# A DLRM tower with ten one-hot tables, gram samples 27 columns apart, whole-bank gram evictions and gram writes by tile

## The chip, the cores and the metric

The kernel runs on one NeuronCore of a Trainium2 chip. The metric is the device time of one execution in microseconds. The core's engines are TensorE (PE in the profile, with its weight loads as PEld), VectorE (DVE), ScalarE (ACT), GpSimd (POOL) and SyncE (SP).

## What is computed

For 2048 samples, 27 rows of 128 numbers are looked up in 27 tables, the 27 × 26 / 2 = 351 dot products of their pairs are formed, and three dense layers follow:

```python
e = jnp.stack([tbl_0[ids[:, 0]], ..., tbl_26[ids[:, 26]]], axis=1)        # 2048 x 27 x 128
interactions = jnp.einsum('bfd,bgd->bfg', e, e).reshape(B, F * F)
z = jnp.concatenate([bottom, interactions[:, TRIL_IDX]], axis=1)          # 128 + 351
h = jnp.concatenate([z, bottom], axis=1)                                  # 607
h = jnp.maximum(h @ W_top1 + b_top1, 0.0)                                 # 512
h = jnp.maximum(h @ W_top2 + b_top2, 0.0)                                 # 256
y = h @ W_top3                                                            # 1
```

Twelve tables have 1000 rows, nine 1250, five 12500 and one 125000. Everything is float32.

## The kernel before

**Halves and tiles.** The batch is worked through in 8 halves of 256 samples (0 to 7; FIRST and LAST in the code), each of two tiles of 128. Halves 0, 1 and 7 are written out, 2 to 6 run in a loop. The dense layers of half i − 1 run inside half i.

**Lookups.** 18 tables are gathered: GpSimd issues one indirect DMA a table and tile (`gather`, L372 to L382), 18 in a run, in groups of four tables, into `rows`. There is one buffer a tile, so the run for tile t of half i + 1 begins when TensorE has transposed the first four tables of tile t of half i (the wait on `built`, L376). TensorE transposes the gathered rows into `embT` (`transpose_tile`, L720). The other 9 tables, all of 1000 rows, stay in SBUF, split into a high and a low part, and are looked up by products with one-hot matrices: VectorE compares ids with row numbers (`make_hot`, L401; a part is 4 instructions of 125 × 256, there are two parts a table and so 18 a half), TensorE multiplies (`onehot_unit`, L702; 8 matmuls a part). Tables go in pairs, the units; unit 4 has one table. The one-hots lie in a ring of `HOT_SLOTS` = 6 parts: part a is made when TensorE has used part a − 6 (L408 to L413). So six parts of the next half are made ahead, inside this half, and 12 are left to its start.

**Order of a half.** `features`: units 0 to 4, with the transposes of tile 0 between them. `first_tile`: pair products of tile 0, u = 0 to 3. `second_rows`: dense layer 1 of the half before (m = 0 to 3), with the transposes of tile 1 between. `second_tile`: pair products of tile 1, with layers 2 and 3 between.

**Pair products.** A matmul takes 4 samples at once: stationary are their 27 columns each, samples 32 apart in `embT`, so 122 columns; moving are their columns 1 to 26, 104 (`pair_products`, L726). 16 matmuls fill two PSUM banks: that is one product u. Two such pairs of banks take turns, so product u ≥ 2 waits until product u − 2 is evicted (L735 to L737). Only the blocks of one sample with itself are of use. Each eviction (`empty_gram`, L420 and L546) copies four of them, 32 partitions × 208: two on VectorE, two on ScalarE, into `gram`, which holds a half.

**Pairs to dense.** When the half is evicted, SyncE writes `gram` to DRAM in two DMAs (`write_gram`, L304) and reads it back feature by sample with 29 DMAs (`read_pairs`, L311), in pieces of 256 bytes. `pairs_high` and `pairs_low` split them in three chunks for layer 1; on ScalarE and VectorE they stand behind the evictions of u = 0, 1, 2 of tile 0. The last half doesn't go through DRAM but is transposed by TensorE.

**SyncE's queue in a half** (`half`, L322): ids of unit 3, gram writes, ids of unit 4, 29 reads, ids of unit 2 for the next half, bottom rows, ids of units 0 and 1 for the next half, store of y. Each load of ids waits until the one-hots from its buffer are made.

## Time and profile before

| | us |
|---|---|
| median of 3 runs | 683.68 |
| lowest, highest | 678.6, 684.86 |
| the profiled execution | 678.93 |
| its span in the profile | 677.1 |
| mean granted TensorE clock | 0.785 of full |

A page of the profile shows one execution: busy times of the engines, DMA queues, the chain of work that ended last, and groups of instructions by source line. The other views are timelines (instructions in order of time, merged where alike), the same chain in order of time, and DMA packets in a stretch. A duration of TensorE's matmuls is modelled, their starts are recorded; when the result is seen to be done is told by the start of whoever waits for it.

### The profile page before, as it was taken

What the parts mean: (1) busy time and instruction counts of PE and PEld (TensorE: products, weight loads), DVE (VectorE), ACT (ScalarE), POOL (GpSimd) and SP (SyncE); (2) the same over time, 40 slices, a digit from 0 to 9 for tenths busy, and PEclk for the clock granted to TensorE, in tenths of its full rate; (3) what the DMA queues carried; (4) which work ended last, traced back from release to release, by engine and by line L of the source; (5) the groups of instructions that cost most, each with busy time, mean ns of one, the idle gap of its engine ahead of it and who ended that gap; (6) DMA issues with size and microseconds to landing.
All of it is one profiled execution on the core that took longest, in us unless ns stands there. A gap on an engine that the chain in (4) does not pass through costs nothing.

```text
span 677.1 us, 9154 instructions
## 1 busy us (share of the span) xinstructions
PE 454.0 (67%) x3110; PEld 430.6 (64%) x3110; DVE 250.0 (37%) x797; ACT 168.6 (25%) x393; POOL 319.0 (47%) x295
## 2 busy tenths in 40 slices
PE   2506575975499274983849838498384974749997
PEld 2406574974488173982849837398373974749987
DVE  5508032932075030741317313173222712228423
ACT  1203121333022040321312213122131212212454
POOL 6775545586607646085450854508454283630000
PEclk9857785985689586985858968698695975859999
DMA  6944512261122301232112341124311261112100
GB/s 165 234 100 90 138 28 58 77 104 44 51 71 63 85 25 47 72 68 78 31 39 72 74 71 31 39 73 73 71 35 35 76 90 51 39 31 78 25 1 1
DMA packets 38113, 44.51 MB, mean 66 GB/s; under 512 B 20127, under 2 KB 30887, under 8 KB 38090
## 3 DMA queue, kind: packets, MB, share of 16 engines
q1 hardware_dynamic: 27251, 23.54, 16.9%
q0 software_dynamic: 9216, 18.89, 10.5%
q10 hardware_dynamic: 1623, 1.79, 1.0%
q8 instruction: 13, 0.21, 0.1%
q14 instruction: 10, 0.08, 0.0%
HBM read 38.50 MB, written 5.69 MB: 65 GB/s over the span
## 4 chain that ended last, share of the span: by engine, by line
PE 45%; another core or an unknown queue 24%; issue 15%; DVE 11%; ACT 2%; DMA 1%; SPq 1%; DVEq 0%; ACTq 0%
PE ps_gram L741 18%; PE ps_dense L750 11%; PE ps_build L714 11%; DVE hot L416 8%; PE ps_build L724 2%; DVE table L395 1%; DMA raw<-tbl_dram 1%; PE ps_dense L787 1%; DVE gram L425 1%; PE ps_gram L750 1%; ACT embT L544 1%; PE ps_gram L724 1%; PE ps_build L750 0%; SPq L277 0%
## 5 line engine op out<-in xcount | busy, mean ns | idle before, releaser
L380 POOL DMA_INDIRECT rows<-tbl_dram,idx x288 | 318.2, 1105 | 281.2 <-issue 110.2
L741 PE MATMUL ps_gram<-embT 128*122 128x104 f32 x1024 | 173.9, 339 | 119.3 <-issue 51.4
L741 PEld LDWEIGHTS ps_gram<-embT 128*122 128x122 f32 x1024 | 163.8, 253 | 129.5 <-issue 77.4
L714 PE MATMUL ps_build<-hot,table 125*128 125x256 f32 x1152 | 154.9, 293 | 46.8 <-issue 32.2
L714 PEld LDWEIGHTS ps_build<-hot,table 125*128 125x128 f32 x1152 | 147.3, 199 | 49.3 <-issue 48.1
L416 DVE TENSOR_SCALAR hot<-id_raw,vocab 125x256 fp32r<-125x256 int32 x576 | 160.8, 354 | 31.4 <-remote 25.5
L425 DVE COPY gram<-ps_gram 32x208 f32<-32x208 f32 x128 | 46.7, 365 | 268.0 <-remote 182.2
L551 ACT COPY gram<-ps_gram 32x208 f32<-32x208 f32 (+1 forms) x128 | 41.4, 324 | 236.1 <-remote 163.3
L750 PE MATMUL ps_dense<-h,w2s 128*128 128x256 f32 x168 | 36.6, 371 | 40.6 <-issue 40.4
L750 PEld LDWEIGHTS ps_dense<-h,w2s 128*128 128x128 f32 x168 | 31.4, 270 | 43.7 <-issue 43.7
L537 ACT COPY embT<-ps_build 128x512 f32<-128x512 f32 (+1 forms) x40 | 24.9, 622 | 135.8 <-PE ps_build L714 79.7
L395 DVE TENSOR_TENSOR h<-ps_dense,h 128x256 fp32r<-128x256 f32 x28 | 11.9, 424 | 101.4 <-ACT h L574 71.3
L750 PE MATMUL ps_dense<-pairT,w1p 120*128 120x256 f32 (+1 forms) x252 | 39.1, 300 | 5.0 <-issue 5.0
L750 PEld LDWEIGHTS ps_dense<-pairT,w1p 120*128 120x128 f32 (+1 forms) x252 | 36.2, 209 | 4.4 <-issue 4.4
L572 ACT ACTIVATE ps_dense<-ps_dense,b1s 128x256 f32<-128x256 f32 x28 | 12.6, 449 | 76.1 <-remote 53.8
L724 PE MATMUL ps_build<-ident,rows 128*128 128x128 f32 x144 | 22.4, 290 | 4.5 <-ACT embT L544 2.6
L724 PE MATMUL ps_gram<-ident,rows 128*128 128x128 f32 x144 | 22.1, 276 | 2.5 <-issue 2.3
L544 ACT COPY embT<-ps_gram 128x512 f32<-128x512 f32 (+1 forms) x40 | 21.5, 545 | 6.7 <-remote 2.9
L544 ACT COPY embT<-ps_build 128x512 f32<-128x512 f32 (+1 forms) x40 | 20.4, 551 | 8.9 <-remote 8.0
L724 PEld LDWEIGHTS ps_build<-ident,rows 128*128 128x128 f32 x144 | 17.6, 149 | 7.5 <-issue 7.4
L750 PE MATMUL ps_dense<-botT,w1b 128*128 128x256 f32 x84 | 19.1, 340 | 0.0
L724 PEld LDWEIGHTS ps_gram<-ident,rows 128*128 128x128 f32 x144 | 16.8, 142 | 3.5 <-issue 3.5
(58 smaller groups left out, 139.2 us busy)
## 6 DMA issues: line engine op xcount, KB each, us to landing
id_raw<-ids_onehot_dram SPq DMA_DIRECT2D x32, 256.0 KB
rows<-tbl_dram,idx POOLq DMA_INDIRECT x288
gram_dram<-gram SPq DMA_DIRECT2D x7, 624.0 KB
raw<-tbl_dram SPq DMA_DIRECT2D x9, 448.0 KB
gram_dram<-gram SPq DMA_DIRECT2D x7, 169.0 KB
id_raw<-ids_onehot_dram SPq DMA_DIRECT2D x8, 128.0 KB
bot<-bottom_dram SPq DMA_DIRECT2D x8, 128.0 KB
w1p_raw<-w_pairs_dram ACTq DMA_DIRECT2D x1, 720.0 KB
```

The source lines that it names most:

```text
L380: nc.gpsimd.indirect_dma_start(rows[:, t, s * D:(s + 1) * D], None, tables[f], bass.IndirectOffsetOnAxis(idx[:, 2 * i + t, f:f + 1], 0)).t ...
L395: return nc.vector.tensor_tensor(dst, whole, high.bitcast(fp32), ALU.subtract)
L416: last = nc.vector.tensor_scalar(hot[0:VP, a % HOT_SLOTS, v, :], id_raw[0:VP, n % ID_SLOTS, q, :], vocab[0:VP, row:row + 1], None, ALU.is_ ...
L425: last = nc.vector.tensor_copy(*gram_pieces(t, u, k))
L537: nc.scalar.copy(embT[:, :, f:f + n], src).then_inc(emb_done, 1)
L544: nc.scalar.copy(embT[:, t * TILE:(t + 1) * TILE, u * FQ:u * FQ + n], src).then_inc(emb_done, 1)
L551: last = nc.scalar.copy(*gram_pieces(t, u, k))
L572: nc.scalar.activation(bank, bank, ACT.Relu, bias=b1s[:, m:m + 1]).then_inc(relu_done, 1)
L714: last = nc.tensor.matmul(bank[:, q * HALF:(q + 1) * HALF], table[0:VP, units[n][q], bits, row:row + D], hot[0:VP, a % HOT_SLOTS, v, :], s ...
L724: last = nc.tensor.transpose(bank[:, f * 128:(f + 1) * 128], rows[:, t, s * D:(s + 1) * D], ident[:, :])
L741: last = nc.tensor.matmul(ps_gram[u % 2][0:GR, c:c + GC], embT[:, at:at + GROUP, :].rearrange("p k g -> p (k g)")[:, 0:GR], embT[:, at:at ...
L750: last = nc.tensor.matmul(bank, w(a), x(b), start=(first and m == 0), stop=(end and m == 2))
```

## The change

- A tenth table is looked up by one-hots: 20 parts a half for 18, 17 gathers a tile for 18. Unit 4 has two tables.
- `HOT_SLOTS` is 5 for 6. Five parts of the next half are made ahead and 15 are left to its start: one instead of two beside layer 1, one behind each eviction of tile 1 as before.
- In halves 0 to 6 samples lie 27 apart in `embT` for 32; the stationary side has 107 columns (4 × 27 − 1) for 122, the moving side 104 as before. The last half keeps the old layout.
- An eviction there is one copy an engine: VectorE takes the whole first bank (107 × 416), ScalarE the whole second, off-diagonal blocks included. `gram` now holds one tile.
- Gram writes go by tile, four DMAs (one a sample of the four) of 26 partitions × 3328 bytes. Those of tile 0 are issued at the end of SyncE's half, ahead of the store of y. The first eviction of tile 1 waits for them, the first of the next tile 0 for those of tile 1.
- The 29 reads have pieces of 128 bytes for 256, eight a row for four.
- The DMA descriptor scratch is 4096 bytes a partition for 8192. In the startup one more table is loaded and split.
- The order of samples in `bottom` and `y` follows the new layout; that costs no work.

```diff
-ONEHOT_TABLES = 9
+ONEHOT_TABLES = 10
-    HOT_SLOTS = 6
+    HOT_SLOTS = 5
+    JT = TILE // GROUP
+    GM = GROUP * FEATURES - 1
...
-        gram = in_arena("gram", [GR, PG, J], fp32, 0)
+        gram = in_arena("gram", [GM, GROUP, PG, JT], fp32, 0)
+        gram_end = in_arena("gram_end", [GR, PG, J], fp32, 0)
...
+        emb_flat = sb("embT", [128, HALF * PAD], fp32)
+        embT_end = emb_flat.rearrange("p (b g) -> p b g", g=PAD)
+        embT = emb_flat[:, 0:HALF * FEATURES].rearrange("p (b g) -> p b g", g=FEATURES)
...
+        TILE_OUT = 16 * GROUP
+        def gram_bank(u, h):
+            src = ps_gram[u % 2][0:GM, h * 512:h * 512 + GB // 2 * GC].rearrange("p (g c) -> p c g", c=GC)
+            j = u * GB + h * GB // 2
+            return gram.rearrange("p k n j -> p (k n) j")[:, :, j:j + GB // 2], src
...
-            def write_gram(i):
-                sp.wait_ge(gram_dve, GRAMS * (i + 1))
-                sp.wait_ge(gram_act, GRAMS * (i + 1))
+            def write_gram(i, t):
+                sp.wait_ge(gram_dve, GRAMS * i + GU * (t + 1))
+                sp.wait_ge(gram_act, GRAMS * i + GU * (t + 1))
                 sp.sem_inc(loads_begun, 1)
-                for a, b in ((0, 96), (96, GR)):
-                    sp.dma_start(scratch[a:b, :], gram[a:b, :, :].rearrange("p n j -> p (n j)")).then_inc(gram_out, 16)
+                for k in range(GROUP):
+                    src = gram[k * FEATURES:k * FEATURES + PG, k, :, :].rearrange("p n j -> p (n j)")
+                    sp.dma_start(scratch[t * GROUP + k, :, :, :].rearrange("r n j -> r (n j)"), src).then_inc(gram_out, 16)
...
             def half(i, at, more=True):
                 next_ids(i, 0, at, 3)
-                write_gram(i - 1)
+                write_gram(i - 1, 1)
                 next_ids(i, 1, at, 4)
                 read_pairs(i - 1, range(len(reads)))
...
                     next_ids(i, 3, at + HALF, 0)
                     next_ids(i, 4, at + HALF, 1)
+                    write_gram(i, 0)
                 store(i - 1, at - HALF)
...
             def empty_gram(i, t, u):
-                if t == u == 0 and not is_half(i, FIRST):
-                    dve.wait_ge(gram_out, 32 * i)
+                if u == 0 and t == 0 and not is_half(i, FIRST):
+                    dve.wait_ge(gram_out, TILE_OUT * 2 * i)
+                if u == 0 and t == 1 and not is_half(i, LAST):
+                    dve.wait_ge(gram_out, TILE_OUT * (2 * i + 1))
                 dve.wait_ge(grammed, GRAMS * i + t * GU + u + 1)
-                for k in (0, 1):
-                    last = nc.vector.tensor_copy(*gram_pieces(t, u, k))
-                last.then_inc(gram_dve, 1)
+                if is_half(i, LAST):
+                    nc.vector.tensor_copy(*gram_pieces(t, u, 0))
+                    nc.vector.tensor_copy(*gram_pieces(t, u, 1)).then_inc(gram_dve, 1)
+                else:
+                    nc.vector.tensor_copy(*gram_bank(u, 0)).then_inc(gram_dve, 1)
...
-                    if more and m < 2:
-                        make_hot(i + 1, m)
+                    if more and m == 0:
+                        make_hot(i + 1, 0)
                 for u in range(GU):
                     empty_gram(i, 1, u)
                     if more:
-                        make_hot(i + 1, 2 + u)
+                        make_hot(i + 1, 1 + u)
...
-                        last = nc.tensor.matmul(ps_gram[u % 2][0:GR, c:c + GC],
-                                                embT[:, at:at + GROUP, :].rearrange("p k g -> p (k g)")[:, 0:GR],
-                                                embT[:, at:at + GROUP, 1:FEATURES], start=True, stop=True)
+                            last = nc.tensor.matmul(ps_gram[u % 2][0:GM, c:c + GC],
+                                                    embT[:, at:at + GROUP, :].rearrange("p k g -> p (k g)")[:, 0:GM],
+                                                    embT[:, at:at + GROUP, 1:FEATURES], start=True, stop=True)
...
-    nc = _bacc.Bacc("TRN2", target_bir_lowering=False, num_devices=1, dynamic_dma_scratch_size=8192)
+    nc = _bacc.Bacc("TRN2", target_bir_lowering=False, num_devices=1, dynamic_dma_scratch_size=4096)
...
-    args["scratch"] = nc.dram_tensor("gram_dram", (128, PG * J), _mybir.dt.float32, kind="Internal").ap()
+    args["scratch"] = nc.dram_tensor("gram_dram", (2 * GROUP, PG, PG, TILE // GROUP), _mybir.dt.float32, kind="Internal").ap()
```

## Rows read from the trace of the kernel before

**Rows 1.** The page: busy time and share of each engine; the gathers' DMA queue.

```profile
PE 454.0 (67%) x3110; PEld 430.6 (64%) x3110; DVE 250.0 (37%) x797; ACT 168.6 (25%) x393; POOL 319.0 (47%) x295
...
q0 software_dynamic: 9216, 18.89, 10.5%
```

**Rows 2.** The chain that ended last, in order of time (start, us, what), half 4.

```profile
379.05 14.69 issue
```

**Rows 3.** Timeline of POOL, half 4 (start, us, engine, line, what, idle before).

```profile
372.23 7.64 POOL L380 DMA_INDIRECT rows<-tbl_dram,idx  x1 [22.35 <-PE ps_gram L724]
380.17 0.94 POOL L380 DMA_INDIRECT rows<-tbl_dram,idx  x1 [0.30 <-PE ps_gram L724]
...
400.15 0.94 POOL L380 DMA_INDIRECT rows<-tbl_dram,idx  x1 [0.30 <-issue]
412.29 0.94 POOL L380 DMA_INDIRECT rows<-tbl_dram,idx  x1 [11.20 <-PE ps_build L724]
...
433.52 0.94 POOL L380 DMA_INDIRECT rows<-tbl_dram,idx  x1 [0.30 <-issue]
```

**Rows 4.** Timeline of DVE, half 4.

```profile
368.46 10.59 DVE L416 TENSOR_SCALAR hot<-id_raw,vocab 125x256 fp32r<-125x256 int32 x40
393.74 0.74 DVE L425 COPY gram<-ps_gram 32x208 f32<-32x208 f32 x2 [14.69 <-issue]
...
404.38 0.74 DVE L425 COPY gram<-ps_gram 32x208 f32<-32x208 f32 x2 [9.09 <-remote]
...
437.91 0.74 DVE L425 COPY gram<-ps_gram 32x208 f32<-32x208 f32 x2 [4.39 <-remote]
```

**Rows 5.** Timeline of PE, half 4.

```profile
363.07 7.91 PE L714 MATMUL ps_build<-hot,table 125*128 125x256 f32 x64
...
384.88 5.31 PE L741 MATMUL ps_gram<-embT 128*122 128x104 f32 x32 [2.33 <-ACT embT L544]
...
405.18 3.62 PE L741 MATMUL ps_gram<-embT 128*122 128x104 f32 x16 [7.01 <-DVE gram L425]
```

**Rows 6.** Timelines of POOL, PE and DVE, half 1.

```profile
134.76 2.67 POOL L380 DMA_INDIRECT rows<-tbl_dram,idx  x1 [0.30 <-issue]
137.73 1.83 POOL L380 DMA_INDIRECT rows<-tbl_dram,idx  x1 [0.30 <-issue]
...
157.70 0.94 POOL L380 DMA_INDIRECT rows<-tbl_dram,idx  x1 [0.30 <-issue]
162.21 0.94 POOL L380 DMA_INDIRECT rows<-tbl_dram,idx  x1 [3.57 <-PE ps_build L724]
...
139.69 8.72 PE L741 MATMUL ps_gram<-embT 128*122 128x104 f32 x64 [3.06 <-ACT embT L544]
...
142.43 0.74 DVE L425 COPY gram<-ps_gram 32x208 f32<-32x208 f32 x2 [3.69 <-issue]
...
148.48 0.74 DVE L425 COPY gram<-ps_gram 32x208 f32<-32x208 f32 x2 [1.90 <-PE ps_gram L741]
...
161.25 0.74 DVE L425 COPY gram<-ps_gram 32x208 f32<-32x208 f32 x2 [11.22 <-remote]
```

**Rows 7.** DMA packets, MB, share, of 139.7 to 146.7 and of 384.9 to 391.9.

```profile
q0 software_dynamic: 32, 0.07, 4.6%
...
q0 software_dynamic: 95, 0.19, 12.1%
```

**Rows 8.** Timelines of POOL and DVE, startup.

```profile
49.42 0.94 POOL L380 DMA_INDIRECT rows<-tbl_dram,idx  x1 [0.30 <-issue]
...
52.48 1.14 DVE L416 TENSOR_SCALAR hot<-id_raw,vocab 125x256 fp32r<-125x256 int32 x4 [14.94 <-remote]
```

**Rows 9.** Timeline of PE, last half, at the full clock.

```profile
633.31 7.07 PE L741 MATMUL ps_gram<-embT 128*122 128x104 f32 x64 [0.74 <-ACT embT L544]
```

**Rows 10.** Timeline of SP, half 4: issues of an id load and of the reads.

```profile
363.31 0.38 SPq L277 DMA_DIRECT2D id_raw<-ids_onehot_dram  x1
...
370.11 11.38 SPq L319 DMA_DIRECT2D pairX<-gram_dram  x29
```

More of the change, by code:

```diff
@@ L351, in _ @@
                     next_ids(0, 0, 0, 3)
-            next_ids(0, 1, 0, 4)
+                if q == 8:
+                    next_ids(0, 1, 0, 4)
             load_bottom(0)
@@ L543, in emb_tile @@
                 src = build_at(s)[:, 0:n * 128].rearrange("p (f b) -> p b f", f=n)
-                nc.scalar.copy(embT[:, t * TILE:(t + 1) * TILE, u * FQ:u * FQ + n], src).then_inc(emb_done, 1)
+                nc.scalar.copy(emb(i)[:, t * TILE:(t + 1) * TILE, u * FQ:u * FQ + n], src).then_inc(emb_done, 1)
             def empty_gram(i, t, u):
-                if t == u == 0 and not is_half(i, FIRST):
-                    act.wait_ge(gram_out, 32 * i)
+                if u == 0 and t == 0 and not is_half(i, FIRST):
+                    act.wait_ge(gram_out, TILE_OUT * 2 * i)
+                if u == 0 and t == 1 and not is_half(i, LAST):
+                    act.wait_ge(gram_out, TILE_OUT * (2 * i + 1))
                 act.wait_ge(grammed, GRAMS * i + t * GU + u + 1)
-                for k in (2, 3):
-                    last = nc.scalar.copy(*gram_pieces(t, u, k))
-                last.then_inc(gram_act, 1)
+                if is_half(i, LAST):
+                    nc.scalar.copy(*gram_pieces(t, u, 2))
+                    nc.scalar.copy(*gram_pieces(t, u, 3)).then_inc(gram_act, 1)
+                else:
+                    nc.scalar.copy(*gram_bank(u, 1)).then_inc(gram_act, 1)
             def bottom_high(i):
@@ L740, in pair_products @@
                         c = b * 512 + g * GC
[L741 to L743 removed]
+                        if is_half(i, LAST):
+                            last = nc.tensor.matmul(ps_gram[u % 2][0:GR, c:c + GC],
+                                                    embT_end[:, at:at + GROUP, :].rearrange("p k g -> p (k g)")[:, 0:GR],
+                                                    embT_end[:, at:at + GROUP, 1:FEATURES], start=True, stop=True)
+                        else:
+                            last = nc.tensor.matmul(ps_gram[u % 2][0:GM, c:c + GC],
+                                                    embT[:, at:at + GROUP, :].rearrange("p k g -> p (k g)")[:, 0:GM],
+                                                    embT[:, at:at + GROUP, 1:FEATURES], start=True, stop=True)
                 if 1 in banks:
@@ L797, in relayout @@
                     for n in range(u * RB, min((u + 1) * RB, PG)):
-                        last = nc.tensor.transpose(bank[0:J, (n % RB) * 128:(n % RB) * 128 + GR], gram[0:GR, n, :],
+                        last = nc.tensor.transpose(bank[0:J, (n % RB) * 128:(n % RB) * 128 + GR], gram_end[0:GR, n, :],
                                                    ident[0:GR, 0:GR])
@@ L878 @@
     gathered, onehot = slots([t.shape[0] for t in tables])
-    bottom = _np.asarray(inputs["r_bottom_mlp_out"]).reshape(HALVES, J, GROUP, D)
+    bottom = _np.asarray(inputs["r_bottom_mlp_out"])
+    by_tile = bottom.reshape(2 * HALVES, TILE // GROUP, GROUP, D).transpose(3, 0, 2, 1).reshape(D, BATCH)
+    by_half = bottom.reshape(HALVES, J, GROUP, D).transpose(3, 0, 2, 1).reshape(D, BATCH)
     w_pairs = _np.zeros((3, CHUNK, H1), w1.dtype)
@@ L883 @@
     layouts = {
-        "bottom": bottom.transpose(3, 0, 2, 1).reshape(D, BATCH),
+        "bottom": _np.concatenate([by_tile[:, 0:LAST * HALF], by_half[:, LAST * HALF:]], axis=1),
         "ids": ids,
```

38 lines of the change are left out of this document (23 added, 15 removed).

## The prediction

> **What bounds the kernel now.** I read the page's busy shares first: no engine is full. TensorE is at 67% of the span, VectorE at 37%, GpSimd, which only issues the table gathers, at 47% in 288 gathers [rows 1]. So waits set the time, and I went to the chain of work that ended last, in half 4 (363.3 to 446.5 us, one of the five halves 2 to 6 that look alike). The chain has a hole there, 14.69 us from VectorE's last one-hot on, that it gives to nobody but "issue" [rows 2]. Beside them I laid the timelines of GpSimd, VectorE and TensorE over the same stretch.
>
> GpSimd gathers in two runs of 18, one a tile of 128 samples. Run A is allowed at 372.23 (TensorE has transposed the old rows), but its first gather takes 7.64 us and ends at 379.87. The rest follow every (400.15 − 380.17)/16 = 1.249 us, up to 401.09. Run B goes from 412.29 to 434.46 [rows 3]. VectorE makes one-hots without a gap from 368.46 to 379.05 [rows 4]: the first gather ends 0.82 us after the last of them. So the one-hots hold run A up.
>
> TensorE's first two pair products of the tile stand at 384.88 to 390.19 [rows 5]. Yet VectorE, idle for 14.69 and then 9.09 us, sees the first as done at 393.74 and the second at 404.38, 3.29 us after run A's end [rows 3, 4]. The next eviction after run B comes at 437.91, again 3.45 us after its end. In half 1 it is 161.25 against 158.64, 2.61 us [rows 6]. In the startup VectorE sits still 14.94 us until 52.48, 2.12 us after the first 36 gathers end [rows 8]. I read this as one thing: while gathers are being moved, the other engines learn late that TensorE is done, and what is pending is let go 2 to 3.5 us after a run ends. What delays the signal I can't say, only that it goes with the gathers.
>
> The kernel is then one ring: run A, its release, third and fourth product and dense layer 1, the first transpose of the second tile, run B, its release, the rest of that tile, the next half's first transpose, one-hots, run A. From the release at 404.38 to run B's start are 7.91 us [rows 3, 4]. Half 1 is different: its four products go through at once (139.69 to 148.41, first and third eviction at 142.43 and 148.48), and run B starts at 162.21, 0.96 us after the release [rows 6]. The table of DMA packets shows what differs. In the 7 us after the first product's start, 32 packets of the gathers' queue were moved in half 1, and 95 in half 4 [rows 7]. One gather is 9216/288 = 32 packets [rows 1]. In half 1 one gather moved, in half 4 three.
>
> **The sum.** It is made against the profiled execution, 678.93 us with a span of 677.1. The median of the three runs is 683.68, so I carry the difference over to that.
>
> *Gathers.* 18 a tile become 17: minus 1.25 us in each of the runs A and B, all on the ring.
>
> *One-hots.* Two more parts of four instructions a half, and with five slots for six one more part is left to the stretch ahead of run A: 13 parts behind the bottom split for 10. A part costs 10.59/10 = 1.06 us [rows 4], so VectorE ends 3.2 us later and run A's first gather at 383.1; run A ends 3.2 − 1.25 = 1.9 us later than now. The Trainium skill ("SBUF — State Buffer", section "SBUF: two separate sides") says that GpSimd can't write its descriptors while a two-port VectorE operation holds their common port. The 7.64 us agree with that; the rule speaks against more one-hots, and would hold run A up by the same 3.2 us.
>
> *TensorE's features.* 16 more matmuls at 7.91/64 = 0.12 us and two transposes less: +1.8 us, ending at 384.4. In halves 0 to 6 run A covers that; in the last half nothing does: +1.8 us.
>
> *Products.* 64 take 7.07 us, 0.11 each at the full clock [rows 9]. If the 122 stationary columns set that pace, 107 make it 0.11 × 107/122 = 0.097; if the 104 moving ones do, nothing is gained. I take the first, as the moving side has fewer columns. At half the clock 16 take 3.62 us [rows 5], about double. Of these, one product of 16 on the ring behind release A (at half clock, 0.4 us) and about three behind release B (0.6 us): −1.0 with a lower end of 0. A gain for the other 64 is covered by the runs.
>
> *Evictions.* One instruction of 416 elements for two of 208. Two take 0.74 us [rows 4]; the one lies between half of that and all of it. I take 0.58. Two on the ring: −0.3, between 0 and −0.7.
>
> *Gram writes.* Eight issues a half for two. The four of tile 0 are issued when its fourth product is evicted (its product ends at 408.80 now, so about 409.6) and are needed at the tile's next eviction, 437.91: 28 us for some 5. On SyncE they stand behind the id loads and ahead of the store of y, which nobody waits for until the next half. The four of tile 1 cost SyncE two issues more of some 0.4 us, while it has to wait for hot part 7 anyway. Cost 0; without that cover, two issues a half, under 1 us.
>
> *Pair reads.* 29 issues as before, but eight pieces of 128 bytes a row for four of 256. They now take 11.38 us of issue [rows 10]. If issuing goes by instruction it stays so, if by pieces it doubles to 22.8. I take the first: a read takes 0.39, with 351 × 4/29 = 48 pieces on average, and an id load of 256 pieces 0.38 [rows 10]. The Trainium skill ("DMA: Bandwidth & Descriptors", section "Why small descriptors are slow (HBM only)") gives each packet a fixed overhead of about three cycles on top of one for 32 bytes; by that the moves alone would take 14/11 = 1.3 times as long, no new term in the sum. No row here has 128-byte packets.
>
> *The smaller descriptor scratch* holds back nothing I can find; the gathers land between one another. If it did, each gather would wait, up to its own 1.25 us. I take 0.
>
> *Startup and half 0.* Two gathers less in the first 36, then one less in each of the two next runs; the tenth table's split and three more parts on VectorE (some 5 us) eat part of the cover of the third run. −3.9 us at the end of half 0's run B, between −5 and 0.
>
> *The order of gathers and products.* This is the large term. Run A's second gather is ready at 384.3 and its third at 385.6, in place of 381.1 and 382.4, while the id loads (issued by SyncE behind the reads, so at the same time) fill the DMA engines. The first product starts at about 385.2. Against the first product's start, the second and third gather are ready at −3.8 and −2.5 us in half 4 now, at −2.3 and −0.1 in half 1 (137.43 and 139.56 against 139.69) [rows 6], and at −0.9 and +0.4 in the new order. So halves 2 to 6 should take half 1's form: products evicted at once, run B 0.96 to 3 us (if the third pair chunk still waits) behind the release. I take 2 in place of 7.91: −5.9.
>
> A half of 2 to 6 is then +1.9 (run A) − 5.9 − 1.25 (run B) − 0.8 = −6.0; without the large term (and with 0.5 more for what lies between release A and run B) −0.7. Half 1: −0.2. The release of the first product varies, so I count four of five: −24.0 − 0.7 − 0.2 − 3.9 + 1.8 = −27.0. 677.1 − 27.0 = 650.1 of span, and 683.7 − 27.0 = **656.7 us**.
>
> **Rivals.**
> 1. *The order stays.* Three gathers still move during the products, because the reads take longer and push the id loads back, or because the signal is lost for another reason. For it: the delay also begins 3 us into run B, where no other DMA runs. Then five times −0.7 − 0.2 − 3.9 + 1.8 = −5.8: 677.9 us.
> 2. *The one-hots break (slower).* If VectorE has to wait for a slot after 372.2, a gather slips in, run A starts inside the features, the signals that free slots come late, and with five slots VectorE stands until the release, as in the startup (14.94 us). A run from 376 ends at 397, is released at 400.4; seven parts, transposes, 64 products and layer 1 take some 17 us: run B at 417.5 in place of 412.3, +5.2 − 1.25 − 0.8 = +3.2 a half, in all +19 − 3.9 + 1.8 = +17: 700.6 us. Against it: a part needs the slot of five parts earlier, which TensorE frees 2.6 us before that (by its 0.96 us a part at 378.6, against 381.2, for the last). It decides when that slack is used up.
> 3. *The lock isn't the cause.* Run A starts as early as today; then 3.2 us a half are saved on top of rival 1: −5.8 − 6 × 3.2 = −25: 658.7 us, the same time by another road. The 0.82 us speak for the lock.
>
> **Chances.** The large term holds: 0.47. Rival 1: 0.30. Rival 2: 0.13. Rival 3: 0.05; the rest is for what I don't see. The range reaches from all five halves in half 1's form with one more us in each (683.7 − 38 = 646) to rival 1 with its small gains lost (684): 646 to 684. The likeliest case has 646 to 664. A measurement here tells about 1% from no change. Faster by over 1% takes the large term, rival 3 and a third of rival 1: 0.62; within 1%: 0.22; slower: 0.16.
>
> **What would show it.** Run A's first gather ends at about 19.8 us from the half's start (now 16.6), 0.8 after VectorE's last one-hot. Runs have 17 gathers, 1.25 us apart. Releases still 3.3 us after them. The second product's eviction stands before run A's end, and run B starts under 3 us after the release. 16 product matmuls in 1.55 us at the full clock. If the second eviction still stands 3.3 us after run A, rival 1 holds. I would be wrong altogether if the late signals had nothing to do with the gathers.

## The result, and the profile after

| | before | after |
|---|---|---|
| median of 4 runs each | 681.68 us | 651.83 us |
| lowest to highest | 678.6 to 684.86 | 641.33 to 657.71 |
| ratio | | 0.9475 (95%: 0.933 to 0.962) |
| profiled execution, its span | 678.93, 677.1 us | 641.33, 639.5 us |
| mean granted TensorE clock | 0.785 | 0.832 |

The ratio leaves disturbed runs out (the profiled one of after_5, 646.44 us, is such a run too); with it 681.68 becomes 645.9 us. Two repetitions gave 637.79 and 639.63 us, ratios 0.952 (0.947 to 0.957) and 0.947 (0.941 to 0.953). I had 656.7 us, 27.0 less than before, in a range of 646 to 684; by the ratio it is 35.8 less, at the fast end of that range. The kernel is 5% faster where I had said 4%.

The page of the changed kernel, busy times and the gathers' queue (beside [rows 1]):

```profile
PE 438.8 (69%) x3222; PEld 412.9 (65%) x3222; DVE 257.7 (40%) x806; ACT 168.9 (26%) x338; POOL 320.9 (50%) x279
...
q0 software_dynamic: 8704, 17.84, 10.9%
```

8704 packets are 272 gathers. Still no engine is full. Half 4 goes from 337.9 to 416.8 us now, 78.9 in place of 83.2. The timeline of GpSimd there (start, us, engine, line, what, idle before), to be read beside [rows 3]:

```profile
347.08 10.91 POOL L400 DMA_INDIRECT rows<-tbl_dram,idx  x1 [21.42 <-PE ps_gram L758]
358.30 0.94 POOL L400 DMA_INDIRECT rows<-tbl_dram,idx  x1 [0.30 <-issue]
...
377.03 0.94 POOL L400 DMA_INDIRECT rows<-tbl_dram,idx  x1 [0.30 <-issue]
384.98 1.02 POOL L400 DMA_INDIRECT rows<-tbl_dram,idx  x1 [7.01 <-PE ps_build L758]
...
405.03 0.95 POOL L400 DMA_INDIRECT rows<-tbl_dram,idx  x1 [0.30 <-issue]
```

And VectorE's, beside [rows 4]:

```profile
343.42 13.74 DVE L436 TENSOR_SCALAR hot<-id_raw,vocab 125x256 fp32r<-125x256 int32 x52
362.11 0.59 DVE L450 COPY gram<-ps_gram 107x416 f32<-107x416 f32 x1 [4.95 <-issue]
...
369.00 0.59 DVE L450 COPY gram<-ps_gram 107x416 f32<-107x416 f32 x1 [5.62 <-remote]
...
380.99 0.59 DVE L450 COPY gram<-ps_gram 107x416 f32<-107x416 f32 x1 [10.72 <-remote]
381.83 0.43 DVE L415 TENSOR_TENSOR pairT<-pairX,pairT 120x256 fp32r<-120x256 f32 x1 [0.25 <-ACT pairT L594]
...
409.26 0.59 DVE L450 COPY gram<-ps_gram 107x416 f32<-107x416 f32 x1 [7.24 <-remote]
```

And TensorE's first three products of the tile, beside [rows 5]:

```profile
360.32 4.77 PE L780 MATMUL ps_gram<-embT 128*107 128x104 f32 x48 [1.12 <-ACT embT L568]
```

Run A's first gather ends at 357.99, 0.83 us after the last one-hot (357.16), and lasts 10.91 us. Two products are evicted ahead of run A's end (377.97) where it was one; the third comes 3.02 us after it, and run B follows that by 3.99 us where it was 7.91. After run B the release is at 409.26, 3.28 us late, as before.

So a half can be read as a ring of four stretches: run A, the gap to run B, run B, the gap to the next half's run A. The next table has them for all kernels of this text, each from one profile. The gaps are means over halves 2 to 6 (the last column: to the end of the first gather of the next half's run A); a half is counted from its first one-hot matmul to that of the next. The last three rows are from another chip, of which more below.

```text
kernel       half 2 starts  mean half 2-6  last half  A's end to B  B's end to A's first gather
before              195.7          83.5        64.0         11.2        28.8
before_2            191.7          82.5        64.0         10.8        28.0
after               177.1          79.4        65.4          7.4        31.2
after_5             186.3          78.6        65.4          6.9        30.7
after_2             181.1          78.6        65.4          6.9        30.7
hot10               186.5          79.7        65.5          7.1        31.3
layout              180.6          81.9        63.6         10.9        27.2
late_run            193.2          80.0        64.0          4.2        32.3
after_late          180.8          81.5        65.5          4.7        35.5
after_u1            185.1          81.5        65.4          0.3        34.8
after_pin           186.3          79.8        65.4          7.1        31.5
no_gather           141.3          45.7        64.0
plain_2             134.9          45.7        64.0          4.9        22.1
spaced_2            140.5          70.4        89.8          1.5         2.3
gap_s               137.8          58.1        78.8          1.2         2.0
gap_4               146.2          58.8        67.6          1.5         2.7
after_gap_s         145.9          60.3        80.5          1.1         2.0
plain               114.0          45.6        64.0          4.9        22.2
spaced              138.4          70.8        89.8          1.5         2.3
after_spaced        140.0          73.9        92.8          1.4         2.3
```

### The profile page after: what moved, and what is told of

It is laid out like the page before. It is cut to its first block, busy times and chain, and to the rows that moved or that the text cites. A ratio compares the mean times of both kernels' runs of the same rounds, so it can differ in the third digit from the quotient of the medians.

```text
span 639.5 us, 9403 instructions
## 1 busy us (share of the span) xinstructions
PE 438.8 (69%) x3222; PEld 412.9 (65%) x3222; DVE 257.7 (40%) x806; ACT 168.9 (26%) x338; POOL 320.9 (50%) x279
## 3 DMA queue, kind: packets, MB, share of 16 engines
q0 software_dynamic: 8704, 17.84, 10.9%
## 4 chain that ended last, share of the span: by engine, by line
PE 55%; issue 19%; another core or an unknown queue 16%; ACT 5%; SPq 3%; DMA 1%; DVE 1%; ACTq 0%
PE ps_build L748 21%; PE ps_gram L780 14%; PE ps_dense L789 11%; PE ps_build L758 3%; PE ps_gram L776 2%; SPq L301 2%; ACT embT L568 2%; PE ps_gram L758 2%; PE ps_dense L826 1%; DMA raw<-tbl_dram 1%; PE ps_gram L789 1%; ACT pairT L594 1%; ACT embT L561 1%; SPq L302 0%
## 5 line engine op out<-in xcount | busy, mean ns | idle before, releaser
L748 PE MATMUL ps_build<-hot,table 125*128 125x256 f32 x1280 | 173.3, 295 | 48.0 <-issue 32.6
L748 PEld LDWEIGHTS ps_build<-hot,table 125*128 125x128 f32 x1280 | 164.9, 200 | 51.5 <-issue 49.3
L436 DVE TENSOR_SCALAR hot<-id_raw,vocab 125x256 fp32r<-125x256 int32 x640 | 177.9, 356 | 36.4 <-remote 22.6
L780 PE MATMUL ps_gram<-embT 128*107 128x104 f32 x896 | 119.6, 293 | 93.9 <-issue 70.2
L780 PEld LDWEIGHTS ps_gram<-embT 128*107 128x107 f32 x896 | 110.1, 204 | 104.5 <-issue 87.5
L450 DVE COPY gram<-ps_gram 107x416 f32<-107x416 f32 x56 | 32.9, 590 | 201.0 <-remote 139.3
L580 ACT COPY gram<-ps_gram 107x416 f32<-107x416 f32 x56 | 28.2, 506 | 186.3 <-remote 145.1
L561 ACT COPY embT<-ps_build 128x512 f32<-128x512 f32 x40 | 32.1, 803 | 147.4 <-PE ps_build L748 80.1
L568 ACT COPY embT<-ps_build 128x512 f32<-128x512 f32 (+1 forms) x40 | 22.8, 609 | 5.7 <-remote 4.8
L789 PEld LDWEIGHTS ps_dense<-botT,w1b 128*128 128x128 f32 x84 | 15.0, 232 | 2.4 <-issue 2.4
## 6 DMA issues: line engine op xcount, KB each, us to landing
gram_dram<-gram SPq DMA_DIRECT2D x56, 84.5 KB
```

What stands on the lines that cost most here:

```text
L436: last = nc.vector.tensor_scalar(hot[0:VP, a % HOT_SLOTS, v, :], id_raw[0:VP, n % ID_SLOTS, q, :], vocab[0:VP, row:row + 1], None, ALU.is_ ...
L450: nc.vector.tensor_copy(*gram_bank(u, 0)).then_inc(gram_dve, 1)
L561: nc.scalar.copy(emb(i)[:, :, f:f + n], src).then_inc(emb_done, 1)
L568: nc.scalar.copy(emb(i)[:, t * TILE:(t + 1) * TILE, u * FQ:u * FQ + n], src).then_inc(emb_done, 1)
L580: nc.scalar.copy(*gram_bank(u, 1)).then_inc(gram_act, 1)
L748: last = nc.tensor.matmul(bank[:, q * HALF:(q + 1) * HALF], table[0:VP, units[n][q], bits, row:row + D], hot[0:VP, a % HOT_SLOTS, v, :], s ...
```

## The experiments

**Which part brings it.** Four kernels in one group on one chip; before: 670.86 us. Theory 1 is that of the prediction, the order of gathers and products; rival 1 is the new layout, rival 2 the fewer gathers.

> The changed kernel once more, in five rounds, as the yardstick for the other kernels of this group. Its own runs went from 641.3 to 657.7 us. Both theories expect a ratio to the kernel before near 0.95, 640 to 655 us.

637.79 us, ratio 0.952.

> The kernel before with the tenth one-hot table alone (five slots, the smaller descriptor scratch, one more load and split in the startup); embT, the products, the evictions and the gram writes are those of before. Theory 1: the gain of the change is one of order, VectorE's one-hots hold GpSimd's gathers up until more of TensorE's products are through and signalled; the layout part only adds about 1 us a half. Then this kernel has the bulk of it: 652 to 662 us, run B 3 to 5 us behind the release of run A in place of 7.9, and halves 0 and 1 some 14 us shorter. Rival 1, the new layout brings it (cheaper products and evictions, writes by tile): this kernel stays at 672 to 680 us. Rival 2, it is only the fewer gathers: 16 x 2 x 1.25 = 40 us at most less what one-hots add; the runs shrink by 1.25 us each and the stretches between them stay as they were, about 678 us.

```diff
-ONEHOT_TABLES = 9
+ONEHOT_TABLES = 10
-    HOT_SLOTS = 6
+    HOT_SLOTS = 5
...
-    nc = _bacc.Bacc("TRN2", target_bir_lowering=False, num_devices=1, dynamic_dma_scratch_size=8192)
+    nc = _bacc.Bacc("TRN2", target_bir_lowering=False, num_devices=1, dynamic_dma_scratch_size=4096)
```

654.26 us, ratio 0.977 (0.973 to 0.982): 16.6 us less. A half is 79.7 us (3.3 less than the mean of the two profiles of before, which are 1.0 apart themselves), run B comes 7.1 us after run A, and run A's first gather takes as long as in the changed kernel:

```profile
355.02 10.80 POOL L381 DMA_INDIRECT rows<-tbl_dram,idx  x1 [21.34 <-PE ps_gram L726]
...
384.94 0.94 POOL L381 DMA_INDIRECT rows<-tbl_dram,idx  x1 [0.30 <-issue]
393.03 1.03 POOL L381 DMA_INDIRECT rows<-tbl_dram,idx  x1 [7.14 <-PE ps_build L726]
```

Half 2 starts at 186.5 us, 5 to 9 us earlier than before and not 14 as said. The 40 us of rival 2 count the gathers twice: there are 16 fewer, at 1.25 us 20 us in all.

> The changed kernel with nine one-hot tables, six slots and the old descriptor scratch: samples 27 apart, 107 stationary columns, whole-bank evictions, gram writes by tile and nothing else. Theory 1: only what stands uncovered on the ring is saved, about 1 us a half, so 672 to 680 us, run B still 7 us behind the release. Rival 1: 645 to 660 us.

```diff
 # the changed kernel, with
-ONEHOT_TABLES = 10
+ONEHOT_TABLES = 9
-    HOT_SLOTS = 5
+    HOT_SLOTS = 6
...
-    nc = _bacc.Bacc("TRN2", target_bir_lowering=False, num_devices=1, dynamic_dma_scratch_size=4096)
+    nc = _bacc.Bacc("TRN2", target_bir_lowering=False, num_devices=1, dynamic_dma_scratch_size=8192)
```

657.78 us, ratio 0.979 (0.972 to 0.987): 13.1 us less, and under the 672 to 680 that theory 1 gave. A half is 81.9 us, 1.1 less, hardly more than the two profiles of before differ by, and run B stands 10.9 us behind run A as before. The rest, over half of the gain, lies ahead of half 2, which starts at 180.6 us.

The two parts add up (16.6 + 13.1 = 29.7 of 33.1 us). In the halves of the loop theory 1 holds: 3.3 us come with the tenth table and 1.1 with the layout. In the startup it fails: the layout alone brings as much there as both together (half 2 starts at 180.6 us, and at 181.5 on the mean of the changed kernel's three profiles). The smaller descriptor scratch goes with the tenth table here; no run has it alone. Rival 2 explains 2.5 us a half and not why the gap from A to B shrinks by 4.

> The kernel before with one wait moved: GpSimd's run A (from half 2 on) waits until one-hot unit 4 of the half is built, in place of the transposes of the first four tables. No operation is added, taken away or made cheaper, and no one-hot is added; run A's first gather ends some 3 to 4 us later. Theory 1: that alone turns the order, the first products go through ahead of the gathers, run B follows the release by 2 to 4 us in place of 7.9, and the kernel is not slower, 667 to 680 us. Rivals: nothing is gained by the order and each half of the ring is 3 to 4 us longer, 700 to 705 us.

```diff
                     if i > 0:
-                        pool.wait_ge(built, BUILDS * (i - 1) + nth("tile", t, u) + 1)
+                        due = nth("hot", 4) if t == 0 and u == 0 and i > 1 else nth("tile", t, u)
+                        pool.wait_ge(built, BUILDS * (i - 1) + due + 1)
```

657.48 us, ratio 0.981 (0.976 to 0.986): 13.4 us less by one later wait, more than expected (667 to 680 us). GpSimd and VectorE, half 4 (354.2 to 435.3 us):

```profile
373.78 0.94 POOL L381 DMA_INDIRECT rows<-tbl_dram,idx  x1 [30.64 <-PE ps_gram L725]
...
395.26 0.94 POOL L381 DMA_INDIRECT rows<-tbl_dram,idx  x1 [0.30 <-issue]
400.31 0.94 POOL L381 DMA_INDIRECT rows<-tbl_dram,idx  x1 [4.11 <-remote]
```

```profile
376.36 0.74 DVE L426 COPY gram<-ps_gram 32x208 f32<-32x208 f32 x2 [6.22 <-PE ps_gram L742]
...
379.51 0.74 DVE L426 COPY gram<-ps_gram 32x208 f32<-32x208 f32 x2 [1.61 <-PE ps_gram L742]
...
389.44 0.74 DVE L426 COPY gram<-ps_gram 32x208 f32<-32x208 f32 x2 [8.38 <-remote]
...
399.36 0.74 DVE L426 COPY gram<-ps_gram 32x208 f32<-32x208 f32 x2 [8.38 <-remote]
```

Run A's first gather ends 20.5 us into the half; without VectorE's one-hots beside it, it takes 0.94 us. Three products are evicted inside it, and run B follows the release by 0.95 us. The order alone, with no operation cheaper, gives 3.0 us a half: 7 from the gap ahead of B, less 3.5 to 4.3 by which A starts later. That the first gather shrinks from 7.6 to 0.94 us shows too that the one-hots hold the gather up (rival 3 of the prediction falls). The one-hots lose nothing by it: 40 instructions take 10.59 us with a gather waiting beside them ([rows 4]) and without.

**Can more of the order be had?** A second group; before: 674.13 us.

> The changed kernel with run A (from half 2 on) held back until one-hot unit 4 is built. Theory: VectorE's one-hots hold run A back already, to 20.2 us from the half's start, so this adds some 2 us to it; the third product is through then, and run B follows the release by 1 us in place of 4. Per half +2 - 3 = -1, in all 0 to 6 us less than the changed kernel. Rival: it only adds its 2 us a half, 10 to 12 us slower.

```diff
 # late_run's wait in the changed kernel
```

661.19 us, ratio 0.985 (0.977 to 0.993): slower than the changed kernel (0.947 to 0.952, in other groups). The theory fell. The gap from A to B is 4.7 for 6.9 us, but the one from B to A is 35.5 for 30.7: 2.4 us are the later start. The other 2.4 lie between run B's end and the half's; I take it that TensorE does there what it had done ahead of run B.

> The changed kernel with run A (from half 2 on) held back until the second pair product of the half is done, some 5 us later than now. Theory: all four products, layer 1's first step and the first transposes of the second tile are then done inside run A, and run B follows it at once (0.3 us) in place of 7: +5 - 7 = -2 a half. Against it, the first transposes of the second tile need the third pair chunk, which may be late; then run B stands where it is and the kernel is 3 to 5 us a half slower.

```diff
+                    if t == 0 and u == 0 and i > 1:
+                        pool.wait_ge(grammed, GRAMS * (i - 1) + 2)
```

663.57 us, ratio 0.985 (0.975 to 0.995). Run B does follow at once (0.3 us), yet it takes 25.4 us for 20 between its first and last gather, and the gap behind it is 4.1 us longer: 2.9 us a half slower, by another road than the one feared. (Both are 81.5 us a half. after_pin, below, is in the same group and has the changed kernel's loop as it is, at 79.8, so up to 1.2 of these 2.9 us can belong to the group.) I read it so: order is worth something only up to the work that fits ahead of a run.

> The changed kernel, with the gathers of half 1's second tile held back until the second pair product of half 0's second tile is done (one wait more, once in the program). Halves 0 and 1 took 177.3 us in one profile of the changed kernel and 186.3 in the other. Theory: this is the same matter of order, decided by chance: whether the four products of half 0's second tile are signalled before the fourth run's signals go late. Pinned, all four are evicted within 6 us, the next run follows at once, and half 2 starts at 176 to 181 us in every execution: 2 to 9 us less than the changed kernel in most runs. Rival: the 9 us have another origin (the startup's loads); then half 2 starts at 186 to 191 and the kernel is 0 to 5 us slower.

```diff
+                    if (i, t, u) == (1, 1, 0):
+                        pool.wait_ge(grammed, GU + 2)
```

650.81 us, ratio 0.967 (0.961 to 0.972). The four evictions came in 5 us and the next run followed by 0.3, as said. But half 2 starts at 186.3 us, what its rival said. The run that was held back starts at 91.7 us (84.2 to 86.7 in the changed kernel's own profiles) and ends at 117.7 (108.7 to 114.3). In it and the next, now back to back, TensorE's one-hot matmuls of half 1 trickle, one every 0.7 to 2.8 us from 109.2 to 126.2. What decides the 9 us between two executions of one and the same kernel in the startup is not settled.

**What the late signals are.** In the same group:

> The kernel before, its table gathers left out from half 1 on (every half uses the rows of half 0, so part of the lookups is not computed); ids, pair reads, gram writes and all else stay. Theory: the late signals go with the gathers. Then each product of the tile is evicted within 1 us of its end, the stretches of 9 to 20 us in which VectorE learns nothing are gone, and a half takes what TensorE is busy in it, 50 to 62 us, in all 450 to 530 us. Rival: the signals are held back by the other transfers of the half (id loads, pair reads); then the second product is still evicted 5 to 10 us late in the stretch of those loads and a half stays over 65 us.

```diff
-            for i in range(1, HALVES):
-                for t in range(2):
-                    gather(i, t)
...
-                pe.wait_ge(rows_in[t][u], 16 * len(bank_slots(u)) * (i + 1))
+                pe.wait_ge(rows_in[t][u], 16 * len(bank_slots(u)))
```

435.51 us. The page, and VectorE in the middle of it:

```profile
PE 375.6 (87%) x3110; PEld 363.4 (84%) x3110; DVE 247.7 (57%) x797; ACT 166.6 (38%) x393; POOL 35.4 (8%) x43
...
PEclk9975559999899999999999999999999999999999
```

```profile
254.81 0.74 DVE L422 COPY gram<-ps_gram 32x208 f32<-32x208 f32 x2 [6.22 <-PE ps_gram L738]
...
256.51 0.74 DVE L422 COPY gram<-ps_gram 32x208 f32<-32x208 f32 x2 [0.16 <-PE ps_gram L738]
...
258.22 0.74 DVE L422 COPY gram<-ps_gram 32x208 f32<-32x208 f32 x2 [0.16 <-PE ps_gram L738]
```

Products are evicted 1.7 us apart, the clock stays up, and a half takes 45.7 us. The id loads and pair reads are all still there. So the late signals do go with the gathers, and with them the kernel loses 37 us a half, more than my theory had (a half of 50 to 62 us without them). Left out with the gathers are the waits for their rows, too; plain_2, below, has rows to wait for and takes the same 45.7 us.

The next group fell on another chip. There **the kernel before took 414.31 us** (412.8 to 415.3, seven runs) with gathers and all, where it took 671 to 682 on the others.

> The kernel before, in which every gather from half 1 on is replaced by a plain DMA of the same 128 rows of 512 bytes on the same GpSimd queue (rows 0 to 127 of the table, not those of the ids, so the lookups are not computed). If the late signals come with any stream of transfers from that queue, they stay: VectorE learns of a product 2 to 4 us after a run's end and a half takes over 75 us if the issues keep the pace of 1.25 us. If they come only with the indirect form, products are evicted within 1 us as without gathers and a half is 46 to 60 us.

```diff
-                        nc.gpsimd.indirect_dma_start(
-                            rows[:, t, s * D:(s + 1) * D], None, tables[f],
-                            bass.IndirectOffsetOnAxis(idx[:, 2 * i + t, f:f + 1], 0)).then_inc(rows_in[t][u], 16)
+                        if i > 0:
+                            pool.dma_start(rows[:, t, s * D:(s + 1) * D], tables[f][0:128, :]).then_inc(rows_in[t][u], 16)
+                            continue
```

> The kernel before, with a small GpSimd memset and a wait for it behind each gather from half 1 on, so that gathers follow every 1.8 to 2.1 us in place of 1.25. Theory A: the late signals depend on how densely gathers come (in one profile of the changed kernel four evictions in half 0 were prompt while VectorE's one-hots stretched single gathers to 1.9, 2.9 and 4.0 us). Then they are prompt here, TensorE's work goes through beside the runs, and a half is two runs of 18 x 1.9 = 34 us, 68 to 75 us in all: 580 to 620 us. Theory B: they come with gathers at any density; then a half grows by 36 x 0.65 = 23 us, 800 to 860 us.

```diff
                             bass.IndirectOffsetOnAxis(...)).then_inc(rows_in[t][u], 16)
+                        if i > 0:
+                            spaces.append(1)
+                            nc.gpsimd.memset(spacer[:, :], 0).then_inc(spaced, 1)
+                            pool.wait_ge(spaced, len(spaces))
```

> The changed kernel with the same spacing. Theory A: 34 gathers a half at 1.9 us, 65 to 72 us a half, 560 to 600 us. Theory B: 34 x 0.65 = 22 us a half more, 770 to 820 us.

408.01, 582.23 (ratio 1.406) and 601.40 us (1.451). Beside 414 us they say nothing on late signals, since that chip has hardly any; they say what the pauses cost: gathers 1.8 us apart (1.94 on the mean) make two runs of 34 us the bound of a half of 70.8 us, and the kernel 41% slower than before. The changed kernel gets 73.9: its one-hots stretch run A to 37 us. So I repeated what matters on the next group, which was of the long sort again (before: 674.96 us).

> The kernel before, for its profile on the chip of this group. Long sort: as in the first profile, 660 to 690 us, a half of 83 to 84 us, the second product's eviction after a run's end. Short sort: 412 to 416 us, all products evicted within 1 us of their end though gathers come every 1.25 us, a half of 45 to 47 us, TensorE busy over 90%.

670.17 us, a half of 82.5 us.

> The changed kernel again, beside the kernel before, on whichever chip this group falls. The last group ran where the kernel before takes 414 us; the earlier ones where it takes 671 to 674. If this group is on a chip of the long sort: 0.945 to 0.96 of before. If it is on one of the short sort, TensorE sets the time: 16 one-hot matmuls more and two transposes less a half cost some 1.8 us, 107 columns for 122 save 128 x 0.013 = 1.7 us in each of seven halves, and the startup has one more table; then 0.99 to 1.02 of before, so the gain of 5% is bound to chips with late signals.

639.63 us, ratio 0.947. The changed kernel was not timed on the chip of 414 us; what the change is worth there stays open.

> Plain DMAs of the same rows in place of the gathers from half 1 on (the lookups of those halves are not computed). On a chip of the long sort: if any stream of transfers from GpSimd's queue brings the late signals, a half is over 75 us; if only the indirect form does, 46 to 60 us and some 410 to 480 us in all. On a chip of the short sort it is 405 to 410 us as before and tells nothing.

428.98 us. The page, then GpSimd's timeline in one half:

```profile
PE 375.9 (88%) x3110; PEld 363.9 (85%) x3110; DVE 248.1 (58%) x797; ACT 167.1 (39%) x393; POOL 210.0 (49%) x295
...
q0 software_dynamic: 9216, 18.89, 16.0%
```

```profile
235.15 16.09 POOL L381 DMA_DIRECT2D rows<-tbl_dram  x18 [15.24 <-PE ps_gram L727]
255.98 9.59 POOL L381 DMA_DIRECT2D rows<-tbl_dram  x18 [4.74 <-PE ps_build L727]
```

The same queue, packets and bytes as in [rows 1], 18 DMAs in 9.59 us, twice as dense as gathers, and a half takes 45.7 us as without any. The first two products are evicted inside run A, 0.31 us behind the start of their last matmul. It is the indirect form that brings the late signals, not the traffic.

> A GpSimd memset and a wait behind each gather, 1.85 us between gathers in place of 1.25. On the short sort it took 582 us, a half of 71 us, which two runs of 34 us set. On a chip of the long sort: if the late signals depend on how densely gathers come, they are prompt and it takes the same 580 to 600 us, less than the kernel before there; if not, 800 to 860 us.

587.66 us, ratio 0.874 (0.868 to 0.880), the time it had on the other chip but for 5 us. Theory A holds: with 1.8 us from gather to gather the signals are prompt, a half is its two runs, and the kernel beats the changed one by 8% though each run is 12 us longer.

**How little of a pause is enough?** The last group; before: 679.73 us.

> The kernel before with a shorter pause behind each gather: a memset of 128 elements in place of 512, about 1.5 us between gathers in place of 1.85. If the signals come promptly at this density too, a half is two runs of 18 x 1.5 + 1.1 = 28 us, 55 to 59 us, and the kernel takes 475 to 510 us on a chip where the kernel before takes 670. If the density is too high, a half is 83 + 36 x 0.28 = 93 us and the kernel takes 730 to 760 us.

```diff
-        spacer = sb("spacer", [128, 512], mybir.dt.uint8)
+        spacer = sb("spacer", [128, 128], mybir.dt.uint8)
```

507.87 us, ratio **0.747** (0.742 to 0.752). The page, and GpSimd:

```profile
PE 407.8 (80%) x3110; PEld 388.9 (77%) x3110; DVE 263.9 (52%) x797; ACT 169.0 (33%) x393; POOL 341.6 (67%) x547
```

```profile
304.53 0.22 POOL L388 MEMSET spacer<- 128x128 uint8 x1
305.02 0.95 POOL L383 DMA_INDIRECT rows<-tbl_dram,idx  x1 [0.27 <-issue]
305.97 0.22 POOL L388 MEMSET spacer<- 128x128 uint8 x1
306.46 0.96 POOL L383 DMA_INDIRECT rows<-tbl_dram,idx  x1 [0.27 <-issue]
307.43 0.22 POOL L388 MEMSET spacer<- 128x128 uint8 x1
308.48 0.95 POOL L383 DMA_INDIRECT rows<-tbl_dram,idx  x1 [0.83 <-issue]
```

From gather to gather it is 1.5 us for most and 1.62 on the mean. A product and its eviction in the same stretch; from the start of the product's last matmul to the eviction it is 0.31 us, as without gathers:

```profile
303.27 1.85 PE L748 MATMUL ps_gram<-embT 128*122 128x104 f32 x16
305.16 0.74 DVE L432 COPY gram<-ps_gram 32x208 f32<-32x208 f32 x2 [1.20 <-PE ps_gram L748]
```

> The kernel before with the long pause (memset of 512 elements, 0.6 us) only behind each group of four gathers (five a run). If one pause in five microseconds lets through what is pending, a half is two runs of 18 x 1.25 + 5 x 0.6 = 25.5 us plus what is learned late by up to 5 us a few times, 52 to 65 us: 460 to 540 us. If the pauses have to be as frequent as the gathers, a half is 83 + 6 = 89 us: 700 to 720 us.

```diff
-                        if i > 0:
+                        if i > 0 and s == bank_slots(u)[-1]:
                             spaces.append(1)
```

509.87 us, ratio 0.748 (0.742 to 0.754). Inside a group of four the gathers keep their 1.25 us. VectorE around the pauses of 306.8 to 308.2 and 316.5 to 317.9 us:

```profile
307.91 0.74 DVE L432 COPY gram<-ps_gram 32x208 f32<-32x208 f32 x2 [2.03 <-remote]
...
317.66 0.74 DVE L432 COPY gram<-ps_gram 32x208 f32<-32x208 f32 x2 [0.98 <-remote]
```

Both evictions come with the end of a pause. I read it so that what is pending is let go in it. In halves 2 to 6 no eviction starts over 3.4 us behind its product's last matmul, where before it was up to 17 us.

> The changed kernel with the shorter pause behind each gather. If the signals are prompt, a half is two runs of 17 x 1.5 + 1.1 = 26.6 us plus what VectorE's one-hots stretch them by: 54 to 60 us, 470 to 510 us, within 2% of gap_s or a little less. If they stay late, 78.6 + 34 x 0.28 = 88 us a half, 700 to 720 us.

529.50 us, ratio 0.778 (0.773 to 0.783): 22 us more than gap_s, where I had said 470 to 510 us. Once the signals are prompt, the change costs: with the tenth table VectorE's one-hots stretch run A to 29 to 32 us (gap_s: 27 to 28), and half 2 starts 8 us later (one profile each).

## Why the prediction was right or wrong

- *What bounds the kernel* (late signals, released 2 to 3.5 us after a run): right, now shown by taking the gathers away. But I took the delay for something given. I costed 27 us around it and did not ask what it costs in all: 240 us.
- *Gathers*: 1.25 us apart, 17 a run. *Products*: in half 4, 48 matmuls in a row took 4.77 us, 0.099 each (0.097 said). *Evictions*: 0.59 us (0.58). *Pair reads*: 29 issues in 11.70 us, so issuing goes by instruction (11.4 said). *Gram writes*: four issues in 1.6 us, and nobody waits for them. *Descriptor scratch*: the cadence hasn't changed.
- *One-hots*: run A's first gather ended 20.1 us into the half for 16.8 before (19.8 for 16.6 said), 0.83 behind VectorE. The rule cited from the Trainium skill ("SBUF — State Buffer", section "SBUF: two separate sides"), that GpSimd can't write descriptors beside a two-port operation of VectorE, agrees: the gather takes 10.9 us when 10.1 us of one-hots are still to come at its start, 7.6 with 6.8, and 0.94 with none.
- *The order*, −5.9 us a half: right in kind, a third too large. Half 4 is +2.1 (half start to run A's end) − 0.3 (release) − 3.9 (release to run B) − 1.2 (run B) − 1.0 (behind it) = −4.3 us. The first product's signal is prompt and the second comes inside run A, as said, but the third only at the release. Behind it stand its eviction, the third pair chunk on ScalarE and VectorE (until 382.26), three matmuls and four transposes, 3.99 us. I had named this case and put it at no more than 3. With the third product through (late_run), run B follows by 0.95 us.
- Nor was the reason right. I had counted how many gathers move beside the products. In half 4 the second and third gather are ready at −1.1 and +0.2 us against the first product (−0.9 and +0.4 said), and still half 1's form did not come. Late_run moves gathers from the first product on, and still its first two products are evicted early and the third inside the run. What goes with the lateness is how long gathers have come densely. From a product's last matmul to its eviction (tile 0 of half 4) it is 0.3 us when the eviction comes 4.1 us behind the end of the run's first gather (after_5), 1.8 at 4.8 us (late_run), 3.3 at 6.2 (after_late), 4.9 at 10.2 (after_5), 7.2 at 13.9 (before). So it counts how many products end in the first few us. No run was made to test this reading.
- *Halves 2 to 6*: −20.5 us against −24.7. The three profiles of the changed kernel and the two of before agree (−3.1 to −4.9 a half).
- *Startup, half 0 and half 1*, −4.1 us: the failed term. In the profile, half 2 starts 18.6 us earlier; over all profiles of either kernel (177.1, 186.3, 181.1 against 195.7, 191.7) it is 12.2, and 14.6 without after_5's 186.3. I applied the order to the loop alone and for these halves counted gathers. Of the two parts of the term, the −3.9 us by the end of half 0's run B are −2.6 in the first pair of profiles and nothing on the mean of all (111.4 against 110.9). It is half 1, put at −0.2, that failed: −15.9 in the first pair, −12.7 on the mean. Most of that is one gap, from the end of half 0's run B to half 1's run A: 12.6 and 12.7 us in the profiles of before, 0.3, 0.3 and 12.6 in those of the changed kernel. I had no such gap in the sum. The products of half 0's second tile meet a run as those of the loop do. Timelines of GpSimd and VectorE, before:

```profile
112.79 0.94 POOL L380 DMA_INDIRECT rows<-tbl_dram,idx  x1 [0.30 <-issue]
126.35 8.11 POOL L380 DMA_INDIRECT rows<-tbl_dram,idx  x1 [12.62 <-PE ps_gram L724]
```

```profile
102.79 0.74 DVE L425 COPY gram<-ps_gram 32x208 f32<-32x208 f32 x2 [5.03 <-remote]
...
116.92 0.74 DVE L425 COPY gram<-ps_gram 32x208 f32<-32x208 f32 x2 [12.21 <-remote]
```

  and after:

```profile
110.15 0.94 POOL L400 DMA_INDIRECT rows<-tbl_dram,idx  x1 [0.30 <-issue]
111.39 0.94 POOL L400 DMA_INDIRECT rows<-tbl_dram,idx  x1 [0.30 <-issue]
```

```profile
93.75 0.59 DVE L450 COPY gram<-ps_gram 107x416 f32<-107x416 f32 x1
...
95.31 0.58 DVE L450 COPY gram<-ps_gram 107x416 f32<-107x416 f32 x1
```

  Before, the third product is evicted at 116.92, behind half 0's run B, and half 1's run A waits 12.6 us. After, all four are out by 95.9, and half 1's run A follows without a gap (the gather of 111.39 is its first). This is part of it and not all: in after_5 only two of them pass and the gap stays, and it gains 9.4 of the 18.6 us. In one profile each, layout closes the gap too (0.3) and hot10 doesn't (12.8). Where it closes, VectorE's one-hots stretch single gathers of this run to 1.9 to 5.0 us (after, after_2 and layout), which breaks the stream as the pauses of gap_s do. Why the layout brings that about, and why in one execution and not in another, stays open.
- *Last half*: +1.4 us (+1.8 said).
- *Rivals*: 1 (the order stays) did not come with the change; it is what layout shows, run B 10.9 us behind run A. 2 (the one-hots break) did not come. 3 fell with late_run.

Together: −4.1 became −12 to −18.6, −24.7 became −20.5, +1.8 became +1.4. The two misses go opposite ways, so that the sum came nearer than its terms is luck.

## What to carry to other kernels

Where a wait is longer than anything that the program asks for, take the suspect away altogether once before tuning around it: one kernel without gathers would have shown 240 us where the change worked for 33. Put work whose completion others need ahead of a long stream of indirect gathers, or break the stream: a 0.2 us memset behind each gather, or a 0.6 us one behind each fourth, made this kernel 25% faster than before, and some 20% faster than the changed one. And time such a kernel on more than one chip. Where the kernel before takes 414 us, a 0.6 us memset behind each gather made it 41% slower; the shorter pauses, 508 and 510 us on their chip, were not timed there. With no late signals, more one-hots were a loss.

## What the runs showed of the hardware

- In all groups but one, other engines learned late of TensorE's finished work while GpSimd issued indirect gathers 1.25 us apart, up to 17 us after a product's last matmul (halves 2 to 6 of before), and what was pending was seen done 3.0 to 3.6 us after the run's last gather (before and before_2). In gather runs of half 4 TensorE itself trickles, one matmul every 1.4 us (the third line follows the release):

```profile
376.73 0.37 PE L789 MATMUL ps_dense<-pairT,w1p 120*128 120x256 f32 x1 [1.02 <-issue]
378.13 0.37 PE L789 MATMUL ps_dense<-pairT,w1p 111*128 111x256 f32 x1 [1.03 <-issue]
...
382.31 1.01 PE L789 MATMUL ps_dense<-pairT,w1p 120*128 120x256 f32 x3 [1.71 <-DVE pairT L415]
```

- It goes with the indirect form (plain DMAs of the same packets: 429 us) and with its density (1.5 us from gather to gather, or a pause after each fourth, 508 and 510 us; 18 in a row at 1.25, 680). Each pause is a memset and a wait for it; whether the time or the wait lets the signals through, no run separates. Which unit is held up, no run tells.
- It is a matter of the chip, or of its state at the time: the kernel before took 414 us in one group and 671 to 682 in the others. The pace of gathers was the same: in half 0, where spaced has no pauses, the first 18 take 23.5 us there and 24.0 in spaced_2, but half 1 starts at 63.6 in place of 84.5 us.
- TensorE's clock is lower where it idles for late signals: mean granted 0.785 before, 0.895 in gap_s, 0.952 without gathers.
- A gather issued while VectorE makes one-hots back to back lasts until 0.8 us after they end: 0.94 us alone, 7.6 and 10.9 with 6.8 and 10.1 us of them still to come.
